# Expert numbers of the second expert layer: loaded with each tile instead of 20 at a time, and three waits fewer per tile

## The chip, the cores and the metric

The kernel runs on one core of a Trainium2 chip. Each engine (TensorE, VectorE, ScalarE, GpSimd, SyncE) has a queue of its own and works through its own program; semaphores order them against each other. The metric is the device time of one execution in microseconds (us).

## The reference

Two transformer layers over 2048 tokens of width 256, in float32. In both, an attention part and an expert part are added to the residual stream. The change lies in the expert part of the second layer: each token goes to 4 of 16 experts.

```
probs = softmax(xt @ w_router)
top_w, top_i = top_k(probs, 4); top_w = top_w / sum(top_w)
g = silu(einsum('td,edh->teh', xt, we1)) * einsum('td,edh->teh', xt, we3)
g = g * cw[:, :, None]                      # cw: top_w at the chosen experts, else 0
moe_out = einsum('teh,ehd->td', g, we2)
shared = silu(xt @ ws1) * (xt @ ws3) @ ws2
out = shared / 5 + moe_out * 4 / 5
```

Here t runs over the 2048 tokens, d over 256, h over 128 and e over the 16 experts.

## The kernel before, in words

The routing sorts the 2048 x 4 pairs of token and expert by expert, and pads each expert's list to whole tiles of 128 rows. That makes 79 tiles (`NT1`), and a row of integers in SBUF, `tile_e`, says which expert each tile belongs to; 8 entries (`EPAD`) stand in front of tile 0's and 24 behind the last tile's. The tokens' rows lie sorted in HBM (`xd`); results go to HBM (`yd`), scattered to the place of their pair.

`stage_experts` works through the 79 tiles as a pipeline over five engines. One call of `tick(j, u)` issues one engine's part for tile j and for the tiles just before it; u is the place of the tile in a body of 16 (`BODY`). On TensorE (function `_(pe)`) a tick has four parts:

- tile j: two transposes of its input rows `xs` into `ps_x` (line 1475);
- tile j-1: the first expert layer, w1 and w3 side by side, `ps_h` (L1484; 256 columns over two halves of the input width, four matmuls in the profile, since float32 goes through in two passes);
- tile j-2: the transpose of its hidden rows into `ps_g` (L1492);
- tile j-3: the second expert layer into `ps_y` (L1499, two matmuls in the profile).

The weights of all 16 experts lie in SBUF. Which expert's weights a matmul reads is given by a register, `bass.ds(e, 1)`; `load_experts` (L1463 to L1466) fills such registers from `tile_e`. Every 16 tiles it loads 20 numbers: for the four tiles before the body and for its 16.

The other engines: SyncE fetches a tile's rows (L1356) into a ring of four (`U`), once the tile four before has been transposed and GpSimd has read its row numbers. ScalarE copies the transposed rows out of PSUM (L1377, signals `x_copied`) and computes silu (L1384). VectorE multiplies (L1401, `hid_ready`), copies the transposed hidden rows (L1408, `g_copied`) and the result (L1416, `y_copied`). GpSimd computes where the rows go (L1448) and scatters them (L1454). All PSUM and SBUF buffers between these steps are double, so before it writes a buffer TensorE waits for the reader of two tiles before: these are the waits in the `since(...)` lines.

`rolled` (L1268 to L1286) sets the order: the first 16 ticks are written out, ticks 16 to 63 are a hardware loop of three rounds with 16 ticks each (`eng.Fori`, L1278), and ticks 64 to 81 are written out again. Before each body it calls `ahead(j)`, which on TensorE is `load_experts`: at j = 0, 16, 32, 48, 64 and 80. In the loop, j is a register.

Behind the stage, all of GpSimd's scatters must have landed; then SyncE and ScalarE fetch the four results per token (L1363, L1390), VectorE and TensorE weigh and add them (L1430, L1517, L1438), and SyncE writes the output. TensorE starts with the shared expert's part for some rows (L1509, L1511) as soon as it has finished the last tile.

Of the kernel before, what the change touches and what calls it, by code (L numbers as in the profile page):

```python
# [32 lines left out]
EPAD = 8  # L33
# [1234 lines left out]
def rolled(eng, lag, tiles, unroll, tick, ahead=lambda j: None):  # L1268

    start = -(-(lag + 2) // unroll) * unroll
    stop = start + (tiles - start) // unroll * unroll
    for j in range(start):
        if j % unroll == 0:
            ahead(j)
        tick(j, j % unroll)
    with eng.Fori(start, stop, unroll) as j:  # L1278
        ahead(j)
        for u in range(unroll):  # L1280
            tick(j + u, u)
    for j in range(stop, tiles + lag):
        if j % unroll == 0:
            ahead(j)
        tick(j, j % unroll)


def stage_experts(nc, m, out):


    tiles, top, xd, yd = NT1, TOP1, m.xd1, m.yd1
    W1 = 2 * HID
    U = YRING
    BODY = 16
    with ExitStack() as ctx:  # L1295
        l = Memory(nc, ctx)
        w1, w2 = m.w13, m.we2
# [3 lines left out]
        xs_t = l.sb("moe1_xs_t", [P, 2, KH, P])  # L1301
        act_out = l.sb("moe1_act", [P, 2, HID])
        hid = l.sb("moe1_hid", [P, 2, HID])
        hid_t = l.sb("moe1_hid_t", [P, 2, P])
# [10 lines left out]
        ps_h = [b[:, 0:W1] for b in bank_h]  # L1315
        ps_g = [b[:, 0:P] for b in bank_g]
        ps_y = [b[:, 0:D] for b in bank_y]
# [10 lines left out]
        x_turned, x_copied = l.sem("moe1_x_turned"), l.sem("moe1_x_copied")  # L1328
        h_done, act_done, hid_ready = l.sem("moe1_h_done"), l.sem("moe1_act_done"), l.sem("moe1_hid_ready")
        g_turned, g_copied = l.sem("moe1_g_turned"), l.sem("moe1_g_copied")  # L1330
# [10 lines left out]
        def there(j):  # L1341

            return not isinstance(j, int) or 0 <= j < tiles

        def since(j, n):

            return not isinstance(j, int) or j >= n

        @block.sync
        def _(sp):  # L1350
            def tick(j, u):
                if there(j):
                    if since(j, U):
                        sp.wait_ge(x_turned, j - (U - 1))
                        sp.wait_ge(home_ready, j - (U - 1))
                    sp.dma_start(xs[:, u % U, :], xd[bass.ds(j * P, P), :]).then_inc(x_in[u % U], 16)  # L1356

            rolled(sp, 0, tiles, BODY, tick)

            for b in range(U):  # L1360
                sp.wait_ge(y_out[b], 16 * len(range(b, tiles, U)))
            for n, i in enumerate(dve_tiles):
                sp.dma_start(yg[i], rows_of(i)).then_inc(fetched[n], 16)  # L1363
            for n, i in enumerate(finish):
                sp.wait_ge(finished, n + 1)
                sp.dma_start(out[0, i * P:(i + 1) * P, :], m.x[:, i, :]).then_inc(stored, 16)
            sp.wait_ge(stored, 16 * T)
# [89 lines left out]
        @block.tensor  # L1457
        def _(pe):
            pe.wait_ge(m.moe1_w_in, 32)

            experts = []

            def load_experts(j):  # L1463
                experts[:] = nc.values_load_multi_w_load_instructions(
                    m.r["tile_e"][0:1, bass.ds(j + (EPAD - U), U + BODY)], engines=[mybir.EngineType.PE], min_val=0,
                    max_val=E - 1, skip_runtime_bounds_check_because=IN_RANGE)[1]  # L1466

            def tick(j, u):
                if there(j):
                    b = u % 2  # L1470
                    pe.wait_ge(x_in[u % U], (j - u % U) * (16 // U) + 16)
                    if since(j, 2):
                        pe.wait_ge(x_copied, j - 1)
                    for k in range(KH):
                        mm = pe.transpose(ps_x[b][:, k, :], xs[:, u % U, k * P:(k + 1) * P], m.ident[:, :])  # L1475
                    mm.then_inc(x_turned, 1)
                if there(j - 1):
                    b = (u - 1) % 2
                    e = experts[U + u - 1]
                    pe.wait_ge(x_copied, j)  # L1480
                    if since(j - 1, 2):
                        pe.wait_ge(hid_ready, j - 2)
                    for k in range(KH):
                        mm = pe.matmul(ps_h[b][:, :], xs_t[:, b, k, :], w1[:, k, bass.ds(e, 1), :],  # L1484
                                       start=(k == 0), stop=(k == KH - 1))
                    mm.then_inc(h_done, 1)
                if there(j - 2):
                    b = u % 2
                    pe.wait_ge(hid_ready, j - 1)
                    if since(j - 2, 2):  # L1490
                        pe.wait_ge(g_copied, j - 3)
                    pe.transpose(ps_g[b][:, :], hid[:, b, :], m.ident[:, :]).then_inc(g_turned, 1)  # L1492
                if there(j - 3):
                    b = (u - 3) % 2
                    e = experts[U + u - 3]
                    pe.wait_ge(g_copied, j - 2)
                    if since(j - 3, 2):
                        pe.wait_ge(y_copied, j - 4)
                    pe.matmul(ps_y[b][:, :], hid_t[:, b, :], w2[:, bass.ds(e, 1), :],  # L1499
                              start=True, stop=True).then_inc(y_done, 1)  # L1500

            rolled(pe, 3, tiles, BODY, tick, load_experts)

            pe.wait_ge(x_copied, tiles)
            pe.wait_ge(hid_ready, tiles)
            for i in range(TAIL_FIRST, T):
                t = i - (T - ON_PE)
                for s in range(HS // P):
                    pe.matmul(ps_sum[t], m.hid_s[:, s, i * P:(i + 1) * P], m.ws2[:, s, :], start=(s == 0), stop=False)  # L1509
                for k in range(KH):  # L1510
                    pe.matmul(ps_sum[t], m.xt2[:, k, i * P:(i + 1) * P], m.wq[:, k, :], start=False, stop=False)  # L1511
            pe.wait_ge(y_copied, tiles)
            pe.wait_ge(diag_ready, 1)
            for t, i in enumerate(pe_tiles):
                pe.wait_ge(fetched[t], 32)
                for k in range(top):
                    mm = pe.matmul(ps_sum[t], diag[:, t, k, :], yg[i][:, k, :], start=(i < TAIL_FIRST and k == 0),  # L1517
                                   stop=(k == top - 1))
                mm.then_inc(combined, 1)
# [460 lines left out]
```

## Time and profile before

| | us |
|---|---|
| median of 3 runs | 945.3 (945.02 to 947.12) |
| the profiled execution | 946.62 |
| its span, first to last instruction | 944.6 |
| TensorE matmul (PE) busy | 864.8 (92%) |
| VectorE (DVE) busy | 642.2 (68%) |
| ScalarE (ACT) busy | 417.2 (44%) |
| GpSimd (POOL) busy | 422.0 (45%) |

The second expert layer's tiles lie between about 771 and 910 us of the span. In the profile PE is TensorE's matmuls and PEld its weight loads, which overlap them. Names that end in q are records of an engine's sequencer: waits (EVENT_SEMAPHORE), register arithmetic (ALU_OP, FUSED_REGOPS), branches, and register loads (TENSOR_LOAD); they don't count as busy time. A record of a sequencer wait begins when the wait is met. Matmuls are pipelined, so their shown durations overlap; the distance between starts is what one costs.

### The profile page before, as it was taken

What the parts mean: (1) busy time and instruction counts of PE and PEld (TensorE: products, weight loads), DVE (VectorE), ACT (ScalarE), POOL (GpSimd) and SP (SyncE); (2) the same over time, 40 slices, a digit from 0 to 9 for tenths busy, and PEclk for the clock granted to TensorE, in tenths of its full rate; (3) what the DMA queues carried; (4) which work ended last, traced back from release to release, by engine and by line L of the source; (5) the groups of instructions that cost most, each with busy time, mean ns of one, the idle gap of its engine ahead of it and who ended that gap; (6) DMA issues with size and microseconds to landing.
All of it is one profiled execution on the core that took longest, in us unless ns stands there. A gap on an engine that the chain in (4) does not pass through costs nothing. (4 is left out here: it accounts for less than half of the span.)

```text
span 944.6 us, 16014 instructions
## 1 busy us (share of the span) xinstructions
PE 864.8 (92%) x4827; PEld 468.3 (50%) x4828; DVE 642.2 (68%) x1528; ACT 417.2 (44%) x739; POOL 422.0 (45%) x719
## 2 busy tenths in 40 slices
PE   5887789899999999999999977789998879999997
PEld 3533223334444444444444321567544667787886
DVE  5589799888788888887888952575714514444466
ACT  3633145465666666665666667222112013333310
POOL 3323065515544336435353464000477826766640
PEclk9998599999999999999999999896999989999999
DMA  9643956421561312911110122640122225555549
GB/s 330 210 131 120 217 113 174 143 45 34 123 176 61 115 46 78 204 45 52 43 50 23 57 66 65 234 162 1 51 100 97 81 76 147 156 152 155 153 164 359
DMA packets 71393, 113.60 MB, mean 120 GB/s; under 512 B 12054, under 2 KB 55318, under 8 KB 70806
## 3 DMA queue, kind: packets, MB, share of 16 engines
q1 hardware_dynamic: 50774, 57.76, 22.2%
q0 software_dynamic: 16000, 45.70, 14.3%
q10 hardware_dynamic: 4544, 9.21, 3.2%
q8 instruction: 38, 0.62, 0.3%
q14 instruction: 37, 0.30, 0.1%
HBM read 58.19 MB, written 54.15 MB: 119 GB/s over the span
## 5 line engine op out<-in xcount | busy, mean ns | idle before, releaser
L1069 DVE TENSOR_REDUCE part_max<-ps_row 128x1 f32<-128x512 f32 (+3 forms) x560 | 353.5, 670 | 69.8 <-PE ps_row L1223 40.5
L939 ACT ACTIVATE probs<-ps_st 128x1024 f32<-128x1024 f32 (+3 forms) x320 | 278.5, 897 | 201.1 <-PE ps_st L1202 199.9
L1127 PE MATMUL ps_o<-probs,v_all 128*17 128x512 f32 (+3 forms) x1280 | 148.5, 536 | 14.4 <-ACT probs L939 8.6
L1223 PE MATMUL ps_row<-ks,qs 96*128 96x512 bf16 (+3 forms) x320 | 109.6, 376 | 12.2 <-DVE part_max L1069 9.0
L1223 PE MATMUL ps_row<-xt_ks,qs 96*128 96x512 bf16 (+3 forms) x320 | 103.1, 350 | 1.0 <-DVE part_max L1069 0.5
L1454 POOL DMA_INDIRECT yd<-moe_ys,moe_home x79 | 78.1, 989 | 44.2 <-POOL moe_home L1448 28.8
L1202 PE MATMUL ps_st<-qs,ks 99*128 99x512 bf16 (+3 forms) x320 | 88.8, 360 | 3.7 <-DMA qs<-max_parts 3.5
L1202 PE MATMUL ps_st<-qs,xt_ks 99*128 99x512 bf16 (+3 forms) x320 | 82.7, 348 | 2.1 <-ACT probs L939 1.3
L1484 PE MATMUL moe_ps_h<-w,moe_xs_t 128*128 x316 | 83.3, 387 | 0.0
L1223 PEld LDWEIGHTS ps_row<-ks,qs 96*128 96x128 bf16 x320 | 31.9, 100 | 94.3 <-DVE part_max L1069 57.3
L1401 DVE TENSOR_TENSOR moe_hid<-moe_ps_h,moe_act 128x128 f32<-128x128 f32 x79 | 23.0, 291 | 76.8 <-ACT moe_act L1384 76.8
L1625 POOL DMA_INDIRECT xd<-xn,slot x64 | 65.9, 1030 | 18.7 <-issue 9.8
L811 POOL TENSOR_SCALAR_AFFINE_SELECT probs<-probs 128x256 f32<-128x256 f32 x128 | 52.4, 416 | 48.9 <-ACT probs L939 47.5
L821 POOL TENSOR_SCALAR moe_h_tanh<-moe_h_tanh 128x128 f32<-128x128 f32 x47 | 24.9, 529 | 96.9 <-ACT moe_h_copy L951 96.6
L1223 PEld LDWEIGHTS ps_row<-xt_ks,qs 96*128 96x128 bf16 x320 | 30.8, 96 | 74.2 <-DVE part_max L1069 40.7
L1377 ACT COPY moe_xs_t<-moe_ps_x 128x256 f32<-128x256 f32 x79 | 29.4, 373 | 76.1 <-PE moe_ps_x L1475 75.8
L1484 PEld LDWEIGHTS moe_ps_h<-w,moe_xs_t 128*128 128x128 f32 x316 | 55.0, 194 | 4.6
L799 POOL DMA_INDIRECT xd<-o_t,slot x32 | 31.3, 977 | 47.3 <-ACT probs L939 42.8
L1127 PEld LDWEIGHTS ps_o<-probs,v_all 128*17 128x17 f32 x1280 | 21.8, 95 | 61.1 <-ACT probs L939 37.1
L1226 PE MATMUL ps_row<-mask,ident 128*128 128x128 bf16 x256 | 50.7, 225 | 0.0
L1202 PEld LDWEIGHTS ps_st<-qs,xt_ks 99*128 99x128 bf16 x320 | 27.4, 98 | 41.9 <-ACT probs L939 21.7
L1499 PE MATMUL moe_ps_y<-we,moe_hid_t 128*128 x158 | 47.2, 382 | 0.0
(266 smaller groups left out, 1329.4 us busy)
## 6 DMA issues: line engine op xcount, KB each, us to landing
moe_xs<-xd SPq DMA_DIRECT2D x79, 129.0 KB, 2.1
xd<-zeros SPq DMA_DIRECT2D x4, 2064.0 KB, 10.3
qk_parts<-probs SPq DMA_DIRECT2D x16, 384.0 KB, 3.3
qs<-qk_parts SPq DMA_DIRECT2D x96, 64.0 KB, 2.5
moe_xs<-xd POOLq DMA_DIRECT2D x47, 128.0 KB, 2.4
yd<-moe_ys POOLq DMA_DIRECT2D x47, 128.0 KB, 2.1
xd<-zeros POOLq DMA_DIRECT2D x2, 2048.0 KB, 15.6
moe_w<-in_w ACTq DMA_DIRECT2D x2, 2048.0 KB, 20.1
```

The costliest lines, as they stand in the source:

```text
L799: pool.indirect_dma_start(out=m.xd0, out_offset=bass.IndirectOffsetOnAxis(m.r["slot"][:, choice, i:i + 1], 0), in_=m.xn[:, i, :], in_offse ...
L811: pool.affine_select(out=corner, in_=corner, compare_op=ALU.is_ge, fill=keep, base=0, pattern=[[0, 2], [1, P]], channel_multiplier=-1).the ...
L939: act.activation(probs[:, at % NPB, :, off:CH], ps_st[at % 2][:, :, off:CH], ACT.Exp, scale=HD ** -0.5).then_inc(exp_done, 1)
L1069: dve.tensor_reduce(part_max[reduced % 2][:, h:h + k, i, j:j + 1], bank[:, 0:k * w].rearrange("p (h w) -> p h w", h=k), AX_X, ALU.max).the ...
L1127: mm = pe.matmul(ps_o[32 * q:32 * q + HD + 1, off:CH], m.v_all[:, k, g * HG + q, :], probs[:, (at + q // 2) % NPB, q % 2, off:CH], start=F ...
L1202: mm = pe.matmul(ps_st[n % 2][:, h, off:CH], ks[g % 2][:, q, k * P:(k + 1) * P], qs[c][:, q, off:CH], start=True, stop=True)
L1223: mm = pe.matmul(cols, qs[c][0:KROWS, h, i * P:(i + 1) * P], ks[g % 2][0:KROWS, h, j * CH:j * CH + w], start=True, stop=(j < c))
L1226: mm = pe.matmul(cols[:, w - P:w], m.ident16[:, :], m.mask16[:, :], start=False, stop=True)
L1454: pool.indirect_dma_start(out=yd, out_offset=bass.IndirectOffsetOnAxis(home[:, k:k + 1].bitcast(U32), 0), in_=ys[:, k % U, :], in_offset=N ...
L1484: mm = pe.matmul(ps_h[b][:, :], xs_t[:, b, k, :], w1[:, k, bass.ds(e, 1), :], start=(k == 0), stop=(k == KH - 1))
L1499: pe.matmul(ps_y[b][:, :], hid_t[:, b, :], w2[:, bass.ds(e, 1), :], start=True, stop=True).then_inc(y_done, 1)
L1625: pool.indirect_dma_start(out=m.xd1, in_=xn[:, i, :], in_offset=None, out_offset=bass.IndirectOffsetOnAxis(r["slot"][:, k, i:i + 1], 0)).t ...
```

## The change

Only TensorE's program of this stage changes. `load_experts` is gone. A tick loads the one number of its own tile, before it waits for the tile's rows, and keeps it for the two matmuls of the next ticks. `load_late`, called where `load_experts` was, loads the numbers of the three tiles before the body again, so that a round of the loop finds them in registers of its own. Three waits are left out of each tick: before the input transposes, the first layer and the hidden rows' transpose. The wait before the second layer stays.

```diff
@@ -1458,48 +1458,46 @@
         def _(pe):
             pe.wait_ge(m.moe1_w_in, 32)
 
-            experts = []
-
-            def load_experts(j):
-                experts[:] = nc.values_load_multi_w_load_instructions(
-                    m.r["tile_e"][0:1, bass.ds(j + (EPAD - U), U + BODY)], engines=[mybir.EngineType.PE], min_val=0,
+            experts = {}
+
+            def experts_of(j, n):
+
+                return nc.values_load_multi_w_load_instructions(
+                    m.r["tile_e"][0:1, bass.ds(j + EPAD, n)], engines=[mybir.EngineType.PE], min_val=0,
                     max_val=E - 1, skip_runtime_bounds_check_because=IN_RANGE)[1]
+
+            def load_late(j):
+                for n, e in enumerate(experts_of(j - 3, 3)):
+                    experts[n - 3] = e
 
             def tick(j, u):
                 if there(j):
                     b = u % 2
+                    experts[u] = experts_of(j, 1)[0]
                     pe.wait_ge(x_in[u % U], (j - u % U) * (16 // U) + 16)
-                    if since(j, 2):
-                        pe.wait_ge(x_copied, j - 1)
                     for k in range(KH):
                         mm = pe.transpose(ps_x[b][:, k, :], xs[:, u % U, k * P:(k + 1) * P], m.ident[:, :])
                     mm.then_inc(x_turned, 1)
                 if there(j - 1):
                     b = (u - 1) % 2
-                    e = experts[U + u - 1]
                     pe.wait_ge(x_copied, j)
-                    if since(j - 1, 2):
-                        pe.wait_ge(hid_ready, j - 2)
                     for k in range(KH):
-                        mm = pe.matmul(ps_h[b][:, :], xs_t[:, b, k, :], w1[:, k, bass.ds(e, 1), :],
+                        mm = pe.matmul(ps_h[b][:, :], xs_t[:, b, k, :], w1[:, k, bass.ds(experts[u - 1], 1), :],
                                        start=(k == 0), stop=(k == KH - 1))
                     mm.then_inc(h_done, 1)
                 if there(j - 2):
                     b = u % 2
                     pe.wait_ge(hid_ready, j - 1)
-                    if since(j - 2, 2):
-                        pe.wait_ge(g_copied, j - 3)
                     pe.transpose(ps_g[b][:, :], hid[:, b, :], m.ident[:, :]).then_inc(g_turned, 1)
                 if there(j - 3):
                     b = (u - 3) % 2
-                    e = experts[U + u - 3]
                     pe.wait_ge(g_copied, j - 2)
                     if since(j - 3, 2):
                         pe.wait_ge(y_copied, j - 4)
-                    pe.matmul(ps_y[b][:, :], hid_t[:, b, :], w2[:, bass.ds(e, 1), :],
+                    pe.matmul(ps_y[b][:, :], hid_t[:, b, :], w2[:, bass.ds(experts[u - 3], 1), :],
                               start=True, stop=True).then_inc(y_done, 1)
 
-            rolled(pe, 3, tiles, BODY, tick, load_experts)
+            rolled(pe, 3, tiles, BODY, tick, load_late)
 
             pe.wait_ge(x_copied, tiles)
             pe.wait_ge(hid_ready, tiles)
```

## Rows read from the trace of the kernel before

**Rows 1.** Busy time by stretch (us, number of instructions), then clock, DMA share, GB/s
```profile
800.00:824.00 24.00, 24.00 (x135) 20.27 (x134) 11.87 (x44) 9.44 (x30) 16.55 (x29) 1.00 0.51 155
...
852.00:855.00 3.00, 1.82 (x10) 1.28 (x9) 0.82 (x3) 0.65 (x2) 2.11 (x5) 1.00 0.57 171
```

**Rows 2.** Timeline, TensorE, around tiles 16, 32, 64: start, length [idle before <-releaser]
```profile
796.37 0.38 PE L1475 MATMUL moe_ps_x<-ident,moe_xs 128*128 128x128 f32 x2
...
799.12 0.43 PE L1475 MATMUL moe_ps_x<-ident,moe_xs 128*128 128x128 f32 x2 [0.96 <-issue]
...
823.63 0.38 PE L1475 MATMUL moe_ps_x<-ident,moe_xs 128*128 128x128 f32 x2
...
826.59 0.43 PE L1475 MATMUL moe_ps_x<-ident,moe_xs 128*128 128x128 f32 x2 [1.17 <-issue]
...
878.59 0.38 PE L1475 MATMUL moe_ps_x<-ident,moe_xs 128*128 128x128 f32 x2
...
881.24 0.41 PE L1475 MATMUL moe_ps_x<-ident,moe_xs 128*128 128x128 f32 x2 [0.87 <-issue]
```

**Rows 3.** The same timeline around tile 48
```profile
851.10 0.38 PE L1475 MATMUL moe_ps_x<-ident,moe_xs 128*128 128x128 f32 x2
...
852.30 0.60 PE L1499 MATMUL moe_ps_y<-we,moe_hid_t 128*128 x2
854.07 0.43 PE L1475 MATMUL moe_ps_x<-ident,moe_xs 128*128 128x128 f32 x2 [1.18 <-issue]
...
855.80 0.38 PE L1475 MATMUL moe_ps_x<-ident,moe_xs 128*128 128x128 f32 x2
...
857.43 0.38 PE L1475 MATMUL moe_ps_x<-ident,moe_xs 128*128 128x128 f32 x2
```

**Rows 4.** Line L1464, all and tile 32's: ns min/median/max, first and last start
```profile
L1464 PEldq TENSOR_LOAD <-tile_e x6: 1361/1576/1621, 769.4 to 906.4; - x6
...
L1464 PEldq TENSOR_LOAD <-tile_e x1: 1542/1542/1542, 824.8 to 824.8; - x1
```

**Rows 5.** Line L1278, the loop's own operations
```profile
L1278 PEldq ALU_OP  x3: 32/32/32, 824.2 to 879.2; - x3
L1278 PEldq COMPARE_BRANCH  x3: 83/220/233, 824.3 to 879.3; - x3
...
L1278 DVEq MOVE  x1: 36/36/36, 825.9 to 825.9; - x1
```

**Rows 6.** The chain of waits, 905 to 945 us: start, length, what
```profile
918.30 20.46 DMA we<-yd
```

**Rows 7.** Loads of eight numbers in the first expert layer, lines L1242 and L779
```profile
L1242 PEldq TENSOR_LOAD <-tile_e x6: 587/594/778, 194.8 to 463.1; - x6
...
L779 POOLq TENSOR_LOAD <-tile_e x6: 572/580/1147, 179.5 to 467.9; - x6
...
L1242 PEldq TENSOR_LOAD <-tile_e x1: 591/591/591, 357.6 to 357.6; - x1
```

**Rows 8.** Lines of TensorE's tick in a steady tile, 863 to 866 us
```profile
L1491 PEldq EVENT_SEMAPHORE  x2: 51/51/51, 863.5 to 865.1; - x2
...
L1498 PEldq EVENT_SEMAPHORE  x1: 51/51/51, 864.2 to 864.2; - x1
...
L1473 PEldq EVENT_SEMAPHORE  x1: 51/51/51, 864.5 to 864.5; - x1
...
L1475 PE MATMUL moe_ps_x<-ident,moe_xs x2: 272/272/273, 865.6 to 865.7; 128*128 128x128 f32 x2
```

**Rows 9.** Timeline, GpSimd, the last two scatters
```profile
910.26 1.03 POOL L1454 DMA_INDIRECT yd<-moe_ys,moe_home  x1 [0.57 <-DVE moe_ys L1416]
911.59 1.06 POOL L1454 DMA_INDIRECT yd<-moe_ys,moe_home  x1 [0.30 <-issue]
```

**Rows 10.** Timeline, TensorE, the stage's first tile
```profile
771.41 0.69 PE L1475 MATMUL moe_ps_x<-ident,moe_xs 128*128 128x128 f32 x2 [4.90 <-DMA moe_xs<-xd]
```

**Rows 11.** Timeline, TensorE, first layer's stage, at a load of eight
```profile
357.94 0.38 PE L1202 MATMUL ps_st<-qs,xt_ks 99*128 99x256 bf16 x2
```

## The prediction

> **What bounds the kernel now.** I read the busy time by stretch first. Between the boundaries of the 16-tile bodies TensorE is busy without a break; in 3 us around a boundary its busy time falls to 1.82 us [rows 1] (three more such windows look alike). GpSimd, the next busiest, has 16.55 of 24 us. The granted clock is 1.00 there, the 2.4 GHz level, so no term below is a matter of the clock. The timeline of TensorE shows the same in single tiles: the first transpose of a tile follows that of the tile before by 1.63 us (855.80 to 857.43 [rows 3]), but by 2.75, 2.96, 2.97 and 2.65 us at tiles 16, 32, 48 and 64 [rows 2, 3], and there the one after it by 1.73. Against 2 x 1.63 that is a loss of 1.22, 1.43, 1.44 and 1.12 us, together 5.2 us; 0.10 of each is the restart. The profile calls the idle time "issue": TensorE waits for no other engine.
>
> The sequencer's own records name it. Before each of these tiles stands one load of 20 expert numbers, 1.54 to 1.62 us long [rows 4]. For tile 48 it begins at 852.2, when TensorE has work queued until 852.9, and ends at 853.8; the transpose starts at 854.07 [rows 3, 4]. The loop's branch (0.22 us) comes ahead of the load, under the queued work [rows 5].
>
> Does the end of the kernel hang on this stage? By the chain of waits yes: TensorE's second layer of the last tile, VectorE's copy, GpSimd's scatter, its landing, then 20.5 us of gathers and the last sums [rows 6]. No step in it has a fixed start. TensorE's own tail sums also start right behind the last tile and move with it.
>
> **The change part by part.** I sum against the profiled execution, 946.62 us for a span of 944.6. It lies 1.3 us above the median of the three runs, 945.3, to which I carry the difference over.
>
> 1. *What a load costs by its size.* 20 numbers take 1.58 us, 8 numbers on the same engine 0.59 [rows 4, 7]: 0.079 and 0.074 per number. The slope between them, 0.082, leaves nothing for a fixed part. So three numbers are 0.24 and one is 0.08. For one number the trace has no row: from below I bound it by 0.03 (a register operation of the loop [rows 5]), from above by 0.59, the whole row of eight. I take 0.08, as both rows lie on a line through zero.
>
> 2. *What stands at a boundary afterwards*: a load of three, then the tile's own load of one, 0.32 together. The second is one more instruction, and the sequencer takes about 0.11 for each (L1473 at 864.5, four more, L1491 at 865.1 [rows 8]): 0.10 between the loads, and in the rolled loop 0.11 for one address operation, which I suppose. That makes 0.53 in the loop, 0.42 in the written-out tiles from 64 on. As long as TensorE still runs dry it restarts earlier by just the difference of the loads, and it can't gain more than that boundary's loss. Tile 16: 1.62 - 0.53 = 1.09 (of 1.22). Tile 32: 1.54 - 0.53 = 1.01. Tile 48: 1.58 - 0.53 = 1.05. Tile 64: 1.62 - 0.42 = 1.20, capped at 1.12. Sum 4.3.
>
> 3. *The boundary at 80*, after the last tile has entered. Its load, from 906.4 to 908.0 [rows 4], holds up the last transpose of hidden rows and the last two second layers by some 0.6 us. Little of it reaches the end: GpSimd waits 0.57 us before its last scatter but one, for VectorE's copy, and 0.30 before the last, where it is itself the bound [rows 9]. So at most 0.57 - 0.30 = 0.27 goes; I take 0.2, the low end is 0.
>
> 4. *The boundary at 0.* The load runs from 769.4 for 1.36 us, to 770.8; the first tile's rows arrive at 771.4 [rows 4, 10]. Hidden, worth 0. While the pipeline fills, some tiles take a load behind waits of their own; I allow 0.2 us of loss in the range.
>
> 5. *A load in every tile, 79 of them.* In a steady tile the sequencer waits too: it passes L1491 at 863.5 and L1498 at 864.2 [rows 8], held by the wait for hidden rows ahead of L1498. The new load would stand where L1473 stands, at 864.5; the transposes behind it start on TensorE at 865.6 [rows 8]. So 1.0 us covers it, against 0.08 + 0.11 + 0.11. Cost 0; even 0.59 with the same additions, 0.81, is covered. That a load holds up nothing that is queued is seen in the first layer: at 357.6 one of eight takes 0.59 us, and matmuls start at 357.94 within it [rows 7, 11].
>
> The Trainium skill speaks against this part. "DMA: Bandwidth & Descriptors" (Latency and other measured facts) gives a tensor load a floor of about 600 ns, and "Runtime: NRT & Kernel Launch" (Instruction fetch mechanics) about 200 ns a register. The second doesn't fit here: eight numbers would take 1.6 us and take 0.59 [rows 7]. The first can't be refuted by the row of eight; by it one number would cost as much as eight, and that is the first rival below, whose time comes from the row.
>
> 6. *Three waits per tile go* (L1473, L1482, L1491), 0.05 us each and 0.11 in the sequencer's pace. Each asks for a count for which the tile before has already waited, so none can hold. They lie in the time in which the sequencer would wait anyway: gain 0, and 0.3 us more cover for the load.
>
> 7. *What is late next.* ScalarE and VectorE go through their own branch at the same boundary; VectorE's last register operation for it is at 825.9 [rows 5]. Without a gap tile 32's transpose would be at 823.63 + 1.63 = 825.26, and VectorE's next work comes over 1 us behind it, since ScalarE's copy or four first-layer matmuls stand between. Hidden. GpSimd needs 1.33 us from the last scatter but one to the last [rows 9] and is asked for 1.63. For the rest the boundary becomes like a steady tile, and a steady tile waits for nothing. No term.
>
> Sum: 4.3 + 0.2 = 4.5 us. The profile's 946.6 becomes 942.1, the median 945.3 becomes **940.8**.
>
> **Bounds.** If the loads cost next to nothing and the restart goes too, all losses go: 5.2 + 0.2, 939.9. If a load of up to four costs 0.30 (8 and 20 numbers as two and five groups of four), a boundary is 0.81 or 0.70: gains 0.81, 0.73, 0.77, 0.92 and 0.2, in all 3.4, 941.9.
>
> **The rivals.**
> - *A load has a fixed price*: one and three numbers cost 0.59 each, like eight. For it: the row of eight, and that 20 may be three such pieces (3 x 0.53). Against it: 0.079 and 0.074 per number. A boundary is 1.39 in the loop, 1.28 outside; the gains 0.23, 0.15, 0.19, 0.34 and 0.2 give 1.1 us, **944.2**.
> - *The gain is lost behind the stage*: TensorE finishes earlier, but scatters or gathers don't end earlier. Against it: GpSimd has a third of its time free [rows 1], and the gathers start with the last scatter [rows 6]. For it: what follows is as long as 18 tiles and belongs to other resources, and a second chain beside the one shown could lie close to it. **945.2**.
> - *The per-tile load breaks its cover* (the slower case). Its place is L1473, the point from which it decides 1.0 us between there and the transpose. One of six loads of eight took 1.15 us on GpSimd instead of 0.58 [rows 7]. If one number on TensorE took that, with 0.22 beside it, each tile would be late by 0.3 us: 75 x 0.3 = 23 us, with no gain at the boundaries: **968**; just past the point, 0.1 us too long, it is 7.5 us, 953. Against it: of TensorE's own six loads of eight none was over 0.78.
> - *The load isn't what the change says*, and more operations come with it: 0.1 us for each at a boundary, within the range, as long as the cover of point 5 holds.
>
> **How the numbers follow.** Cost by the number 0.63 and groups of four 0.13 (both faster), fixed price 0.12 and gain lost behind 0.06 (both within 0.2%, 1.9 us, about what a measurement of this kernel tells from no change), cover broken 0.06. Faster 0.76, same 0.18, slower 0.06. The range takes in the fixed price, and below the bound of 939.9 the 0.3 us by which runs scatter: 939.6 to 944.3. It leaves out the broken cover and the lost gain.
>
> **What would show it.** The spacing of first transposes at tiles 16, 32, 48 and 64 falls to 1.6 to 2.0 us, all others stay at 1.63. Loads of three take 0.24, of one 0.08. No records of waits at what were L1473, L1482 and L1491. The last scatter starts near 907.1 instead of 911.6, and the gathers still take 20.5 us. The prediction is wrong if steady tiles take more than 1.63 us, if one number costs over 0.3 us, or if the last scatter moves and the end doesn't.

## The result, and the profile after

| | before | after |
|---|---|---|
| median of 20 runs, us | 946.48 (944.71 to 948.90) | 944.76 (942.91 to 947.71) |
| ratio, 95% interval | | 0.998 (0.9971 to 0.9989) |
| profiled execution, its span | 946.62, 944.6 | 942.91, 941.1 |
| first transpose of tile 4 to start of the last scatter | 133.12 | 131.67 |

The change makes the kernel faster by 1.9 us (1.0 to 2.7), forecast were 4.5. Ratios, here and below, leave out two executions of other versions, of 1044 and 1267 us, in which the granted clock fell to 0.82 and 0.65.

The two profiled spans differ by 3.5 us, but the one after is of the fastest of its 20 runs: 1.39 us of the 3.5 lie ahead of the stage (first transpose at 770.02 instead of 771.41), 0.35 in its first tiles, 0.3 behind the last scatter. The stage, taken from tile 4's first transpose to the start of the last scatter, gives the other 1.45 us; that is the number to explain. In two profiles of the kernel after it repeats to 0.13 us; before was profiled once.

The timeline of TensorE around tile 48, to be laid beside [rows 3] (after, L1479 is the transposes, L1485 the first layer, L1497 the second):

```profile
848.92 0.38 PE L1479 MATMUL moe_ps_x<-ident,moe_xs 128*128 128x128 f32 x2
...
850.11 0.60 PE L1497 MATMUL moe_ps_y<-we,moe_hid_t 128*128 x2
851.66 0.43 PE L1479 MATMUL moe_ps_x<-ident,moe_xs 128*128 128x128 f32 x2 [0.95 <-issue]
...
853.34 0.38 PE L1479 MATMUL moe_ps_x<-ident,moe_xs 128*128 128x128 f32 x2
...
854.97 0.38 PE L1479 MATMUL moe_ps_x<-ident,moe_xs 128*128 128x128 f32 x2
```

The gap is still there: 0.95 us of "issue" instead of 1.18. Tile 48 follows by 2.74 us instead of 2.97, the next by 1.68 instead of 1.73. Steady tiles are at 1.63 as before. Against 2 x 1.63 the losses at tiles 16, 32, 48 and 64 are 1.04, 1.17, 1.17 and 0.72; they were 1.22, 1.43, 1.44 and 1.13 [rows 2, 3]. That is 1.13 us of the 1.45. The rest, 0.31, comes at the end, from the last tile's transpose to the last scatter: 7.45 to 7.14 us. Not all of it is the load at tile 80: this stretch took 7.33 in a second profile of after, and 7.33 too in the kernel before without its waits, which keeps the load of 20; in eight versions below, with a short load at 80 or none, it is 7.14 to 7.20.

What stands in the gap now, by the loads' own line (the late load of three numbers and tile 48's own, then all 80 that the trace has, then the late load at 80), beside [rows 4]:

```profile
L1465 PEldq TENSOR_LOAD <-tile_e x1: 993/993/993, 850.0 to 850.0; - x1
...
L1465 PEldq TENSOR_LOAD <-tile_e x1: 305/305/305, 851.2 to 851.2; - x1
...
L1465 PEldq TENSOR_LOAD <-tile_e x80: 296/302/1055, 768.1 to 903.5; - x80
...
L1465 PEldq TENSOR_LOAD <-tile_e x1: 770/770/770, 903.5 to 903.5; - x1
```

A load of one number takes 0.30 us, not 0.08, and one of three takes 0.99 (0.77 at tile 80), not 0.24. From the start of the first to the end of the second stand 1.5 us where one load of 1.58 stood. Three numbers cost more than eight did in [rows 7] (0.59).

The last scatters, beside [rows 9]:

```profile
907.12 0.98 POOL L1454 DMA_INDIRECT yd<-moe_ys,moe_home  x1 [0.30 <-issue]
908.40 1.02 POOL L1454 DMA_INDIRECT yd<-moe_ys,moe_home  x1 [0.30 <-issue]
```

GpSimd no longer waits for VectorE's copy ahead of either. In the chain of waits the gathers take 20.42 us, as before [rows 6]; the end moved with the last scatter:

```profile
914.87 20.42 DMA we<-yd
```

### The profile page after: what moved, and what is told of

Its sections match the earlier page's. It is cut to its first block and busy times, and to the rows that moved or that the text cites. A ratio compares the mean times of both kernels' runs of the same rounds, so it can differ in the third digit from the quotient of the medians.

```text
span 941.1 us, 15887 instructions
## 1 busy us (share of the span) xinstructions
PE 863.5 (92%) x4827; PEld 467.7 (50%) x4828; DVE 642.3 (68%) x1528; ACT 417.0 (44%) x739; POOL 422.0 (45%) x719
## 5 line engine op out<-in xcount | busy, mean ns | idle before, releaser
L1485 PE MATMUL moe_ps_h<-w,moe_xs_t 128*128 x316 | 82.9, 386 | 0.0
L1485 PEld LDWEIGHTS moe_ps_h<-w,moe_xs_t 128*128 128x128 f32 x316 | 55.0, 194 | 4.7 <-issue 0.3
L1497 PE MATMUL moe_ps_y<-we,moe_hid_t 128*128 x158 | 47.2, 382 | 0.0
```

The costliest lines, as they stand in the source:

```text
L1497: pe.matmul(ps_y[b][:, :], hid_t[:, b, :], w2[:, bass.ds(experts[u - 3], 1), :], start=True, stop=True).then_inc(y_done, 1)
```

## The experiments

The runs on sizes, with three or four numbers in each own load, and with two loads per tile stand against a median of before of 946.9 us; the others were made on a chip where it is 979.7. The difference lies ahead of this stage: there the first transpose of after begins at 802.81 instead of 770.02. So I compare by the ratio to before on the same chip, and by the stage from tile 4's first transpose to the last scatter, which is nearly the same on both (after 131.67 and 131.80). What lies behind the last scatter varies by up to 1.9 us from profile to profile (32.2 to 34.1), so ratio and stage need not agree to the microsecond. "Losses" adds up, for tiles 16, 32, 48 and 64, the distance to the tile before and that of the next tile, less 2 x 1.63. The "own load" is the one that a tick makes for its own tile; the "late load" is that of `load_late`.

| kernel | ratio to before (95%) | losses | stage, us |
|---|---|---|---|
| before | | 5.23 | 133.12 |
| after | 0.998 (0.9971 to 0.9989) | 4.10 | 131.67 |
| after once more | 0.998 (0.9958 to 1.0003) | 3.98 | 131.80 |
| four late numbers | 0.9951 (0.9933 to 0.9970) | 1.62 | 129.42 |
| four late numbers, own load last | 0.994 (0.9922 to 0.9957) | 0.07 | 127.72 |
| three late numbers, own load last | 0.9955 (0.9935 to 0.9974) | 2.05 | 129.74 |
| after with the waits | 1.0011 (0.9996 to 1.0027) | 4.59 | 132.17 |
| before without the waits | 0.9994 (0.9980 to 1.0009) | 4.59 | 132.35 |
| four late, own last, with the waits | 0.9953 (0.9935 to 0.9971) | 0.49 | 128.39 |
| three numbers in each own load | 1.0079 (1.0058 to 1.0101) | 5.63 | 137.96 |
| four numbers in each own load | 1.0111 (1.0091 to 1.0131) | 4.78 | 144.58 |
| two loads per tile, no late load | 0.9963 (0.9949 to 0.9977) | 0.92 | 129.97 |
| 19 numbers instead of 20 | 1.0331 (1.0306 to 1.0356) | 25.61 | 161.25 |

**Four late numbers instead of three.** The trace after suggested that a load works in groups of four. (The diffs show only the changed lines; ... stands for lines between them.)

```diff
-                for n, e in enumerate(experts_of(j - 3, 3)):
-                    experts[n - 3] = e
+                for n, e in enumerate(experts_of(j - 4, 4)):
+                    experts[n - 4] = e
```

> The kernel after, with one size changed: ahead of each body four numbers are loaded instead of three (the first of them is not used). Theory, pieces of four: a load costs 0.30 us for each whole group of four numbers and 0.30 to 0.35 for each number left over (1: 0.30, 3: 1.0, 8: 0.59, 20: 1.58). Then the load of four takes 0.30 instead of 0.99 to 1.06, the first transposes of tiles 16, 32 and 48 come 0.69 earlier each, that of tile 64 at most by its whole remaining loss of 0.7; in all 2.8 us less than the kernel after, 4.3 less than before. Rival, small loads cost 0.33 per number: four take 1.3, each boundary loses 0.3 more, 1.2 us slower than the kernel after. Rival, the boundary is held by something else (branch, instruction fetch): the load gets shorter and the transposes stay where they are, no change against the kernel after.

The timeline around tile 48 and the late load there:

```profile
884.42 0.38 PE L1479 MATMUL moe_ps_x<-ident,moe_xs 128*128 128x128 f32 x2
...
886.52 0.43 PE L1479 MATMUL moe_ps_x<-ident,moe_xs 128*128 128x128 f32 x2 [0.30 <-issue]
```

```profile
L1465 PEldq TENSOR_LOAD <-tile_e x2: 304/326/348, 885.5 to 886.1; - x2
```

The late load of four (the row's longer one, 0.35) takes a third of the time of three, and the idle time falls from 0.95 to 0.30. The stage is 2.25 us shorter than after, where 2.8 were expected. Both rivals fall. One number more makes the stage shorter.

**The tile's own load at the end of its tick.** Its number is first needed a tick later, so ahead of the transposes it is only in the way.

```diff
-                    experts[u] = experts_of(j, 1)[0]
                     pe.wait_ge(x_in[u % U], (j - u % U) * (16 // U) + 16)
...
                     pe.matmul(ps_y[b][:, :], hid_t[:, b, :], w2[:, bass.ds(experts[u - 3], 1), :],
                               start=True, stop=True).then_inc(y_done, 1)
+                if there(j):
+                    experts[u] = experts_of(j, 1)[0]
```

> As the run with four late numbers, and the tile's own load moved from the head of its tick to the end of it (it is first used a tick later), so that at a boundary only the load of four stands ahead of the transposes. Pieces of four: the loss that is left at a boundary falls to 0.1 us or less; 3.9 us less than the kernel after, 5.4 less than before, the best version. If own load and its address operation cost nothing at the boundary: the same as the run with four late numbers. Steady tiles 1.63 by both. If a load behind the second layer delays the next transposes, steady tiles rise above 1.63.

```profile
883.12 0.38 PE L1478 MATMUL moe_ps_x<-ident,moe_xs 128*128 128x128 f32 x2
...
884.74 0.41 PE L1478 MATMUL moe_ps_x<-ident,moe_xs 128*128 128x128 f32 x2
...
886.39 0.38 PE L1478 MATMUL moe_ps_x<-ident,moe_xs 128*128 128x128 f32 x2
```

Tile 48 (884.74) now follows like any other, 1.62 us behind the tile before, and no row has idle time. The stage is 5.4 us shorter than before and 3.95 shorter than after, as expected (5.4 and 3.9), and the ratio agrees (0.994 of 979.7 is 5.9 us less, 4.2 to 7.6; the plain medians differ by 4.5). This version beats both kernels.

**The same with three late numbers**, to part the two moves.

> The kernel after with the tile's own load at the end of its tick, the late load of three stays. Ahead of the boundary's transposes then stands 1.0 us of load instead of 1.0 + 0.15 + 0.30. The loss at tiles 16, 32 and 48 falls from 1.04 to 1.17 to about 0.5, at 64 from 0.72 to about 0.2; stage 2.4 us shorter than after. Together with the run with four late numbers this says which of the two moves pays how much. If the own load costs a boundary nothing: as after.

```profile
883.88 0.43 PE L1478 MATMUL moe_ps_x<-ident,moe_xs 128*128 128x128 f32 x2 [0.50 <-issue]
```

At tile 48 the idle time is 0.50 us, where after has 0.95. Stage 129.74: 1.9 us less than after, for moving the own load alone, against 2.25 for the fourth number alone and 3.95 for both. The expectation was 2.4; losses of 0.70 and 0.72 are left at 32 and 48, for the load of three.

**Sizes and starts of a load.** The own load in written-out tiles with other sizes, of which only the first number is used: `size(j)` is 1 to 15 for tiles 64 to 78, 1 to 8 for the first tiles, and 1 in the loop. The tile's index in `tile_e` is its number plus 8. One execution, read for its loads alone.

```diff
-                    experts[u] = experts_of(j, 1)[0]
+                    experts[u] = experts_of(j, size(j))[0]
```

> The kernel after with other sizes of the tile's own load in the written-out tiles, of which only the first number is used: tile 64 loads 1, tile 65 loads 2, and so on to 15 at tile 78; tiles 1 to 14 load 2, 3, 4, 2, 3, 4, 5, 2, 3, 4, 8, 2, 3, 4. Read from the loads' durations. Pieces of four (0.30 each, each number left over 0.30 to 0.35): 1: 0.30, 2: 0.65, 3: 1.0, 4: 0.30, 5: 0.6, 6: 0.95, 7: 1.3, 8: 0.6, 9: 0.9, 12: 0.9, 15: 1.9. A straight line by the number of numbers through 1 and 3: 4: 1.35, 8: 2.7. If the start address has to be a multiple of four numbers too, the loads of four at tiles 3, 6, 9 and 14 cost 1.3.

The line of the loads, tile by tile. In this order: 5 numbers from index 15 (tile 7), then 1 from 72, 2 from 73, 3 from 74, 4 from 75, 5 from 76, 6 from 77, 8 from 79, 9 from 80, 12 from 83, 13 from 84, 15 from 86.

```profile
L1465 PEldq TENSOR_LOAD <-tile_e x1: 1490/1490/1490, 783.4 to 783.4; - x1
...
L1465 PEldq TENSOR_LOAD <-tile_e x1: 311/311/311, 883.2 to 883.2; - x1
...
L1465 PEldq TENSOR_LOAD <-tile_e x1: 654/654/654, 884.1 to 884.1; - x1
...
L1465 PEldq TENSOR_LOAD <-tile_e x1: 1019/1019/1019, 885.8 to 885.8; - x1
...
L1465 PEldq TENSOR_LOAD <-tile_e x1: 1272/1272/1272, 887.4 to 887.4; - x1
...
L1465 PEldq TENSOR_LOAD <-tile_e x1: 602/602/602, 889.3 to 889.3; - x1
...
L1465 PEldq TENSOR_LOAD <-tile_e x1: 1712/1712/1712, 891.0 to 891.0; - x1
...
L1465 PEldq TENSOR_LOAD <-tile_e x1: 2118/2118/2118, 896.1 to 896.1; - x1
...
L1465 PEldq TENSOR_LOAD <-tile_e x1: 852/852/852, 898.9 to 898.9; - x1
...
L1465 PEldq TENSOR_LOAD <-tile_e x1: 3021/3021/3021, 906.8 to 906.8; - x1
...
L1465 PEldq TENSOR_LOAD <-tile_e x1: 1277/1277/1277, 910.4 to 910.4; - x1
...
L1465 PEldq TENSOR_LOAD <-tile_e x1: 3811/3811/3811, 916.3 to 916.3; - x1
```

The expectation held only with its last sentence. Where the start is a multiple of four (72, 76, 80, 84), a whole group of four costs about 0.3 and each number left over another 0.3: 5 take 0.60, 9 take 0.85, 13 take 1.28. From any other start there are no groups: 12 take 3.02 and 15 take 3.81, 0.25 each; the short ones take up to 0.35 a number (3 from index 74 take 1.02, 7 from index 78 take 2.20). Size and start change together in tiles 64 to 78, so pairs of one size have to part them: five numbers take 0.60 from index 76 and 1.49 from index 15, eight take 0.59 from multiples of eight ([rows 7]) and 2.12 from index 79. All loads of before start at multiples of four with a multiple of four numbers. The late load of after starts at index j + 5, which is none; the fourth number of the first experiment moved its start to j + 4 as well. That the start counts is shown; whether the engine or the built instruction makes the groups is not.

**Four numbers in each tile's own load**, the same rule in the loop.

```diff
-                    experts[u] = experts_of(j, 1)[0]
+                    experts[u] = experts_of(j, 4)[0]
```

> The kernel after with four numbers in each tile's own load, one of them used. By pieces of four it takes 0.30 as one number does: steady tiles 1.63, the same time as the kernel after. By a price per number it takes 1.3 and is slower still than the run with three (25 us or more).

This expectation, too, knew nothing of the start, and it missed: 10.5 us slower than before by the ratio. The line's loads and the timeline at tiles 68 to 72:

```profile
L1465 PEldq TENSOR_LOAD <-tile_e x80: 332/1120/1257, 770.5 to 919.2; - x80
```

```profile
899.36 0.38 PE L1479 MATMUL moe_ps_x<-ident,moe_xs 128*128 128x128 f32 x2
...
901.17 0.41 PE L1479 MATMUL moe_ps_x<-ident,moe_xs 128*128 128x128 f32 x2
...
902.95 0.41 PE L1479 MATMUL moe_ps_x<-ident,moe_xs 128*128 128x128 f32 x2
...
904.74 0.41 PE L1479 MATMUL moe_ps_x<-ident,moe_xs 128*128 128x128 f32 x2
...
906.39 0.38 PE L1479 MATMUL moe_ps_x<-ident,moe_xs 128*128 128x128 f32 x2
```

Here the last distance is tile 72's, whose numbers start at 80: its load takes 0.34 and the distance is 1.65. The three before it have loads of 1.15 to 1.24 and distances of 1.78 to 1.81. Every fourth tile of the stage has such a short load.

**Three numbers in each tile's own load**, where does the cover end?

> The kernel after with three numbers in each tile's own load, one of them used. By pieces of four the load takes 1.0 us, with its address operation 1.1 to 1.2, against a cover of 1.0: every steady tile takes 1.75 to 1.85 us instead of 1.63, 9 to 17 us slower than the kernel after. If my cover of 1.0 us is too small (sequencer further ahead than I read), steady tiles stay at 1.63 and the boundaries alone cost 0.7 each, 3 us slower.

The loads of tiles 34 (in the loop), 70 (written out) and 64 (whose three numbers start at 72), and the transposes of tiles 33 and 34:

```profile
L1465 PEldq TENSOR_LOAD <-tile_e x1: 763/763/763, 832.9 to 832.9; - x1
...
L1465 PEldq TENSOR_LOAD <-tile_e x1: 765/765/765, 896.9 to 896.9; - x1
...
L1465 PEldq TENSOR_LOAD <-tile_e x1: 787/787/787, 887.2 to 887.2; - x1
```

```profile
831.93 0.42 PE L1479 MATMUL moe_ps_x<-ident,moe_xs 128*128 128x128 f32 x2
...
833.73 0.43 PE L1479 MATMUL moe_ps_x<-ident,moe_xs 128*128 128x128 f32 x2
```

Three numbers take 0.79 from a multiple of four too: they are no group. In the written-out tiles the load takes about 0.77 and the tiles stay at 1.63; in the loop it takes 0.76 to 1.02, and tiles take 1.67 to 1.88. Not its length alone decides: tile 34's load is as short as tile 70's, but in the loop more register operations stand ahead of it, it begins 0.97 us behind the last tile's transposes instead of 0.69, and the tile takes 1.80. The run is 7.5 us slower than before by the ratio, 4.8 us in the stage (6.3 slower than after); against after 9 to 17 were expected, for loads of 1.0 throughout.

**Two loads per tile and no late load.**

```diff
-            rolled(pe, 3, tiles, BODY, tick, load_late)
+            rolled(pe, 3, tiles, BODY, tick)
...
+                    e = experts_of(j - 1, 1)[0]
                     pe.wait_ge(x_copied, j)
...
+                    e = experts_of(j - 3, 1)[0]
                     pe.wait_ge(g_copied, j - 2)
```

> No load ahead of a body at all: each tick loads one number for the first layer (tile j-1) and one for the second (tile j-3), each just before its use. Two loads of 0.30 per tile with an address operation each, 0.8 us in all against a cover of 1.0: steady tiles 1.63. At a boundary nothing stands ahead of the transposes but the branch, and the first layer waits for one load of 0.30: the loss falls to 0.1 to 0.2 us, 3.5 to 3.9 us less than the kernel after. If each load really takes more of the tick than its duration, the load between hidden rows and second layer shows: steady tiles 1.65 or more, and each 0.05 us costs 4 us.

```profile
850.15 0.38 PE L1475 MATMUL moe_ps_x<-ident,moe_xs 128*128 128x128 f32 x2
...
851.78 0.38 PE L1475 MATMUL moe_ps_x<-ident,moe_xs 128*128 128x128 f32 x2
...
853.78 0.38 PE L1475 MATMUL moe_ps_x<-ident,moe_xs 128*128 128x128 f32 x2
```

3.15 us shorter than before in the stage, 1.7 shorter than after, where 3.5 to 3.9 were expected. Tiles 16, 32, 48 and 64 themselves follow by 1.63 (48 is at 851.78), the tile behind three of them by 1.78, 2.02 and 2.01, and 1.4 us more are lost in other tiles (18, 28 and 69). I suppose that two loads per tick leave no room to catch up; no run shows what holds these tiles.

**The three waits**, put back into the kernel after, left out of the kernel before, and put back into the best version:

```diff
+                    if since(j, 2):
+                        pe.wait_ge(x_copied, j - 1)
...
+                    if since(j - 1, 2):
+                        pe.wait_ge(hid_ready, j - 2)
...
+                    if since(j - 2, 2):
+                        pe.wait_ge(g_copied, j - 3)
```

> The kernel after with the three waits per tile put back. Theory (a wait that can't hold costs nothing, since the sequencer waits 0.67 us per tile for the hidden rows): the same as the kernel after within its scatter, steady tiles at 1.63, boundaries as after to 0.1 us. Rival (the waits made room that the load of each tile needs): steady tiles above 1.63, each 0.1 us of it 7.5 us in all.

> The kernel before with only the three waits per tile left out; the loads of 20 stay. Theory: the same as before, boundaries at 2.75 to 2.97 us to 0.1 us, steady tiles 1.63. Rival (the gain of the change comes from the waits): 1.5 us faster than before.

> Four late numbers and the own load at the end of the tick, and the three waits per tile put back. Theory: the waits cost 0.5 to 0.8 us in all only because TensorE runs dry at boundaries and the sequencer then issues without cover; here it does not run dry, so the waits cost nothing: stage as in the run without them (127.7 us from tile 4's transpose to the last scatter, to 0.2 us). Rival (the waits cost at every boundary whatever stands there): 0.5 us or more longer, 128.2 and up.

The stage says the same three times: with the waits it is longer by 0.50, 0.77 and 0.67 us. The total times say it less well: before without the waits is at 0.9994, its interval reaches 1; after with the waits is 1.9 us slower in its median than after on the same chip, more than the stage explains, and that rest is open. In steady tiles the waits cost nothing, 1.63 in all three. The cost is nearly all at the boundaries (losses changed by 0.49, 0.64 and 0.42; in the third run 0.3 more went at tiles 66 and 67). The kernel before without them, around tile 48 (compare [rows 3]):

```profile
884.52 0.38 PE L1473 MATMUL moe_ps_x<-ident,moe_xs 128*128 128x128 f32 x2
887.38 0.43 PE L1473 MATMUL moe_ps_x<-ident,moe_xs 128*128 128x128 f32 x2 [1.07 <-issue]
889.07 0.38 PE L1473 MATMUL moe_ps_x<-ident,moe_xs 128*128 128x128 f32 x2
```

The gap is 1.07 instead of 1.18, with one wait less ahead of the transposes, and the tile behind follows by 1.69 instead of 1.73, with one less ahead of the first layer. At tiles 16, 32 and 64 the transposes come 0.08, 0.08 and 0.16 earlier; each load of 20 differs by up to 0.07 from its like in before, so the price of one wait isn't known closer than that. My theory for the third run, that waits cost nothing where TensorE doesn't run dry, fell: losses rose from 0.07 to 0.49. With a load of only 0.35 the waits still show at tiles 16, 32 and 48.

**Nineteen numbers instead of twenty in the kernel before.** If the start decides, leaving out the unused first number must hurt.

```diff
-                    m.r["tile_e"][0:1, bass.ds(j + (EPAD - U), U + BODY)], engines=[mybir.EngineType.PE], min_val=0,
+                    m.r["tile_e"][0:1, bass.ds(j + (EPAD - U + 1), U + BODY - 1)], engines=[mybir.EngineType.PE], min_val=0,
```

The two places that read the registers count one less accordingly.

> The kernel before, but each load of 20 numbers becomes one of 19: its first number, which is never used, is left out, so that the load starts one entry later, at an index that is no multiple of four. Theory now (aligned groups): from a start that is a multiple of four a load takes 0.30 per group of four and 0.25 to 0.30 per number left over; from any other start all its numbers are taken one by one, 0.25 each. Then 19 numbers take 4.8 us instead of 1.6, each of the boundaries 16, 32, 48, 64 and 80 loses 3.2 us more, the stage's start some 2 us: 16 to 19 us slower than before. Rival (groups of four from any start, numbers left over one by one): four groups and three singles, 2.0 us, 2 us slower. Rival (price by the number alone): 0.08 less per boundary, no change.

```profile
L1464 PEldq TENSOR_LOAD <-tile_e x6: 4512/5206/5243, 801.8 to 965.7; - x6
```

5.2 us instead of 1.58: the theory came near with 4.8, and both rivals fall. But the kernel is 32 us slower (1.0331; 28.1 in the stage), not 16 to 19. Timeline and windows around tile 32 (in the windows the last three figures are granted clock, DMA share, GB/s):

```profile
865.03 0.38 PE L1475 MATMUL moe_ps_x<-ident,moe_xs 128*128 128x128 f32 x2
...
871.62 0.69 PE L1475 MATMUL moe_ps_x<-ident,moe_xs 128*128 128x128 f32 x2 [4.80 <-issue]
...
874.87 0.64 PE L1475 MATMUL moe_ps_x<-ident,moe_xs 128*128 128x128 f32 x2
...
877.73 0.38 PE L1475 MATMUL moe_ps_x<-ident,moe_xs 128*128 128x128 f32 x2
```

```profile
864.00:866.00 2.00, 2.00 (x13) 1.70 (x12) 1.01 (x4) 0.84 (x3) 1.52 (x4) 1.00 0.53 144
...
874.00:877.00 3.00, 3.00 (x10) 2.25 (x9) 0.91 (x3) 0.65 (x2) 0.60 (x1) 0.50 0.01 4
877.00:895.00 18.00, 18.00 (x100) 15.29 (x99) 9.03 (x33) 7.14 (x22) 12.27 (x22) 0.99 0.47 141
```

Behind the idle 4.80 us the granted clock is 0.50, 1.2 GHz, and the next tiles take 3.25 and 2.86 us instead of 1.63. Behind the gaps of 0.95 to 1.18 us in after and before the clock stays at 1.00. By the two distances in "losses" each boundary lost 5.1 us more than before, 3.6 of it the load and 1.5 the slow tile. The third distance (2.60, 2.86 and 3.02 behind tiles 16, 32 and 48) adds 3.6 us in all, and 4.2 are lost behind the last tile's transpose, where the load at 80 keeps GpSimd waiting 4.77 us for VectorE's copy. The expectation had nothing for the clock. The remaining 4 of the 32 us lie outside the stage as I measure it.

**After once more**, on the slower chip:

> The kernel after, unchanged, on the chip of the three others: 131.7 us from tile 4's transpose to the last scatter as in its first profile, 1.5 us less than before; and 4.0 us slower than the run with four late numbers and own load last.

Ratio and stage repeat (0.998, 131.80); against the best version it is 4.08 us longer in the stage.

## Why the prediction was wrong

- *Bound.* Right. Every experiment that changed the gaps at the boundaries moved the stage the same way, by the losses and what other tiles added, and the whole kernel with it. Only for the waits do the total times say little.
- *Point 1, what a load costs by its size.* This step failed. I priced one number at 0.08 and three at 0.24 from a line through 8 and 20 numbers; they cost 0.30 and 0.77 to 1.06, so that 1.5 us stand at a boundary where the sum had 0.53. The line was good only for what it was drawn through: loads that start at a multiple of four and are a multiple of four long. I had written down groups of four as a bound, but let three numbers count as one group, which they aren't, not even from a multiple of four (0.79), and I never asked where the loads start, which the code tells.
- *Point 2, the sum at the boundaries.* It follows from point 1: 4.3 us forecast, 1.13 measured. Of the 1.13 the waits give 0.5 to 0.6 (losses 5.23 to 4.59 without them, 4.59 to 4.10), the loads the other half. Tile 64, where no address operation stands, gives most (0.41).
- *Point 3.* Right in mechanism: GpSimd's wait for the copy is gone. The stretch is 0.31 shorter, 0.2 were forecast; a second profile of after gives 0.12.
- *Point 4.* Right for the first tile: its load begins at 768.1 and its rows come at 770.02. How long the next three take varies by more (6.71 and 7.28 us to tile 4 in two profiles of after) than their loads could cost.
- *Point 5, the cover of the per-tile load.* Right: steady tiles stay at 1.63, though the load took 0.30 instead of 0.08. Three numbers each show that 0.77 is still covered in written-out tiles and no longer in the loop, where more register operations stand beside it; a cover of 1.0 for all of them together fits that.
- *Point 6, the waits.* Wrong by 0.5 to 0.8 us. They cost nothing in a steady tile; but a boundary has no cover, and there one wait less ahead of the transposes brought them forward by 0.08 to 0.16.
- *Point 7.* Right, as far as the best version goes: with the gaps closed, losses are 0.07 and nothing else came late.
- *The rivals.* The fixed price came nearest by its number (1.1 us), for a wrong reason: a load of one costs half of 0.59, one of three up to nearly twice as much. The lost gain forecast a time as near (945.2), but what it says didn't happen: the last scatter came earlier and the end with it. The broken cover didn't come either; its own sum is off, since 1.15 + 0.22 is 0.37 beyond 1.0, not 0.3, which makes 28 us and not 23. The floor of about 600 ns that the Trainium skill gives ("DMA: Bandwidth & Descriptors", Latency and other measured facts) isn't seen; the shortest load took 0.30. The same row says that the compiler unrolls by four to spread it, and four is the size of the groups measured here, though no run shows that the two are the same thing; I had read it and not used it.
- *The level.* My time was 945.3 minus the gain. The median of before over 20 runs is 946.5, so 1.2 us of the miss of 4.0 are the three runs I started from.

## What to carry to other kernels

A price taken from a line through two sizes holds for sizes and starts like these; before using it for one or three, ask what all the measured ones have in common. These register loads want a start and a length that are multiples of four, even if that loads a number that nobody uses: four aligned numbers took 0.35, three took 0.77 or more, and 19 took 5.2 where 20 took 1.58. Work that a steady loop hides costs its full time at the loop's edge, so put there only what the next instruction needs.

## What was not expected of the hardware

- A load of registers from SBUF by TensorE's sequencer: 0.30 us for one number (a few right behind a boundary up to 0.56), 0.33 to 0.38 for one aligned group of four, 0.24 to 0.35 for each number of an unaligned load; 20 numbers 1.58 us, 19 numbers from one entry later 5.2.
- Behind 4.8 us without work TensorE was granted 0.50 of its clock for the two tiles that followed; behind 1.2 us it kept 1.00.
- A sequencer wait that is already met, 0.05 us long in the trace, costs about 0.1 us where TensorE has run dry, and nothing in a steady tile.
